# Layer-norm statistics of the linear attention taken on VectorE during the experts, its rows shared by VectorE and ScalarE

## The reference, cut to what matters

```python
x = L0_attn_x                                                   # (4, 1024, 256)
x = x + _L0_attn_ref(_layernorm(x, axis=-1), W_Q, W_K, W_V, W_O)
x = x + _L0_ffn_ref(_layernorm(x, axis=-1), ...)                # 32 experts of 128 x 128, latent width 128
x = x + _L1_attn_ref(_layernorm(x, axis=-1), ...)               # linear attention, 16 heads of 128
x = x + _L1_ffn_ref(_layernorm(x, axis=-1), ...)                # 48 kept experts, capacity 96

def _layernorm(x, axis=-1, eps=1e-05):
    m = jnp.mean(x, axis=axis, keepdims=True)
    v = jnp.var(x, axis=axis, keepdims=True)
    return (x - m) / jnp.sqrt(v + eps)
```

## Time and profile before

| | |
|---|---|
| time, median of three runs | 2960.62 us (2959.38 to 2962.0) |
| time of the profiled execution | 2959.6 us |
| span of the profiled execution | 2957.0 us |
| PE busy in the span | 2703.8 us, 91% |
| DVE busy | 1668.0 us, 56% |
| ACT busy | 1411.9 us, 48% |
| POOL busy | 789.5 us, 27% |
| phase `experts` (first to last row of DVE) | 802.4 to 1185.8 us |
| phase `lnC` (first to last row of DVE) | 1186.8 to 1222.2 us |
| first matmul of `lin` | 1233.9 us |

### The profile page before, as it was taken

How to read it: one execution, slowest core, us unless ns; L and a number is a source line. 1 busy time by engine, 2 the same in 40 slices (tenths; PEclk the granted TensorE clock), 3 DMA queues, 4 the chain that set the end, 5 groups by cost and what they waited for, 6 DMA issues and landing times. The chain is left out here.

```text
span 2957.0 us, 50661 instructions
## 1 busy us (share of the span) xinstructions
PE 2703.8 (91%) x17706; PEld 2184.6 (74%) x17706; DVE 1668.0 (56%) x3256; ACT 1411.9 (48%) x2605; POOL 789.5 (27%) x808
## 2 busy tenths in 40 slices
PE   7899999979799999599999999999999999986573
PEld 6444444468578888499998989989899998984462
DVE  7688888546588887544444444444444444448321
ACT  6477777856478777433333333333333333327210
POOL 3522221200052222122222222222222222213574
PEclk9799999989899999699999999999999999986666
DMA  8955564030154453300000000000000000004476
GB/s 253 205 98 75 73 81 67 3 98 3 54 223 185 184 184 128 116 1 1 23 1 23 1 20 4 1 23 1 23 1 1 22 1 19 1 20 143 114 166 124
DMA packets 158641, 204.14 MB, mean 69 GB/s; under 512 B 17568, under 2 KB 134976, under 8 KB 149696
## 3 DMA queue, kind: packets, MB, share of 16 engines
q1 hardware_dynamic: 149904, 186.14, 23.7%
q0 software_dynamic: 8544, 15.22, 2.9%
HBM read 154.74 MB, written 50.78 MB: 70 GB/s over the span
## 5 line engine op out<-in xcount | busy, mean ns | idle before, releaser
L1846 POOL TENSOR_TENSOR lin_o2sum<-lin_o2sum,lin_o 128x512 f32<-128x512 f32 x128 | 183.7, 1436 | 1019.5 <-ACT lin_o L1883 1019.5
L875 DVE TENSOR_REDUCE score_pm<-score_SM 128x1 f32<-128x512 f32 (+3 forms) x608 | 364.5, 657 | 80.5 <-PE score_SM L735 47.8
L829 ACT ACTIVATE score_PR<-score_SE 128x512 f32<-128x512 f32 (+1 forms) x640 | 309.8, 558 | 106.3 <-PE score_SE L763 102.6
L2101 DVE TENSOR_TENSOR C_acc<-lin_OUT,C_acc 128x512 f32<-128x512 f32 x256 | 177.1, 692 | 266.3 <-PE lin_OUT L1963 264.6
L2084 DVE SCALAR_TENSOR_TENSOR lin_go<-lin_gT,lin_O 128x512 f32<-128x512 f32 x128 | 88.0, 688 | 421.0 <-PE lin_O L1999 377.2
L1866 ACT ACTIVATE lin_qT<-lin_PJ 128x512 f32<-128x512 f32 x129 | 77.0, 597 | 433.2 <-PE lin_PJ L1925 433.2
L1925 PE MATMUL lin_PJ<-C_XH,lin_WH 128*128 128x512 f32 x774 | 253.8, 409 | 14.0 <-DVE lin_WL L2040 14.0
L1925 PE MATMUL lin_PJ<-C_XL,lin_WH 128*128 128x512 f32 x774 | 241.0, 392 | 0.0
L735 PE MATMUL score_SM<-A_KR,A_QR 96*128 96x512 bf16 (+3 forms) x768 | 229.9, 341 | 12.1 <-DVEq L81 9.4
L1925 PE MATMUL lin_PJ<-C_XH,lin_WL 128*128 128x512 f32 x774 | 240.9, 392 | 0.0
L763 PE MATMUL score_SE<-A_QR,A_KR 99*128 99x512 bf16 (+3 forms) x768 | 210.5, 330 | 2.0 <-ACT score_PR L829 1.5
(11 more groups left out here) (356 smaller groups left out, 6609.9 us busy)
## 6 DMA issues: line engine op xcount, KB each, us to landing
experts_sq<-B_roots SPq DMA_DIRECT2D x64, 1024.0 KB, 4.7
A_QR<-q_parts SPq DMA_DIRECT2D x96, 128.0 KB
A_KR<-k_parts SPq DMA_DIRECT2D x96, 128.0 KB
kept_GU<-L_ffn_gate_up_proj SPq DMA_DIRECT2D x48, 192.0 KB
v_rows<-inp_vt SPq DMA_DIRECT2D x32, 256.0 KB, 4.1
A_V<-v_rows SPq DMA_DIRECT2D x16, 512.0 KB
C_w<-L_attn_w_qkv SPq DMA_DIRECT2D x27, 256.0 KB
q_parts<-inp_parts SPq DMA_DIRECT2D x16, 384.0 KB, 3.6
```

The costliest lines, as they stand in the source:

```text
L829: nc.scalar.activation(PR[:, st % BUFS, h, 0:width], SE[:, e % RING, 0:width], ACT.Exp, scale=SCALE)\
L875: nc.vector.tensor_reduce(pm[:, n % 2, h0:h0 + nh, t, k0 // CHUNK], SM[:, count % RING, 0:nh * nk].rearrange("p (h k) -> p h k", h=nh), AX ...
L1846: nc.gpsimd.tensor_tensor(o2sum[:, c], o2sum[:, c], o2[:], ALU.add).then_inc(pool_sum, 1)
L2101: nc.vector.tensor_tensor(dst, OUT[:, half], dst, ALU.add).then_inc(dve_acc[half], 1)
```

## The change

`experts`: DVE's loop over the chunks is written out in Python, so that its semaphore counts are constants. After `low` at e = 14, 17, 20 and 23 it takes `bn_stats` of one tile of the previous chunk, and at e = 27 the four `bn_aggr`. The results `mv` and `stats` are in a PSUM tensor, `C_mv`, that lives on into `lnC`. At g = 0 the "previous chunk" is chunk 7, whose statistics are taken again later.

`lnC`: `normalise_phase` takes the place of `transpose_phase`. ACT loads the table for the root first. DVE computes the variances and scales of chunks 0 and 1 from what is there, takes the statistics of chunk 7 (`bn_stats` between variances and scales, `bn_aggr` behind the first rows), and then does the 24 tiles that are left in one go. Of each chunk's four tiles of rows ACT makes two and DVE two, both for chunk g + 2 right behind their share of chunk g. The nine DMAs of SP stay, and so do the transposes and the two buffers.

```diff
-            with dve.Fori(0, CHUNKS) as g:
+            for g in range(CHUNKS):
                 for e in range(E):
                     weigh(g, e)
@@
+                    if e in STATS_AT:                      # (14, 17, 20, 23)
+                        j = STATS_AT.index(e)
+                        t = (g + CHUNKS - 1) % CHUNKS * TPC + j
+                        dve.wait_ge(dve_x, done(2 * g + 1))
+                        dve.wait_ge(dve_mv, done(g * TPC - 1))
+                        nc.vector.bn_stats(stats[:, j, :], X[:, t, :]).then_inc(dve_stats, 1)
+                    if e == MEANS_AT:                      # 27
+                        dve.wait_ge(dve_stats, done(g * TPC + TPC - 1))
+                        for j in range(TPC):
+                            t = (g + CHUNKS - 1) % CHUNKS * TPC + j
+                            nc.vector.bn_aggr(mv[:, t, :], stats[:, j, :]).then_inc(dve_mv, 1)
@@ lnC, DVE
-            if norm:
-                variances(0)
-                scales(0)
-                variances(1)
-            for g in range(CHUNKS):
-                ... scales(run), variances(run + 1) ...
-                make_low(g)
+            variances(0)
+            for j in range(TPC):
+                nc.vector.bn_stats(stats[:, j, :], X[:, tile_of(CHUNKS - 1, j), :]).then_inc(stats_ready, 1)
+            scales(0)
+            make_rows(0)
+            dve.wait_ge(stats_ready, TPC)
+            for j in range(TPC):
+                nc.vector.bn_aggr(mv[:, tile_of(CHUNKS - 1, j), :], stats[:, j, :]).then_inc(mv_ready, 1)
+            dve.wait_ge(mv_ready, TPC)
+            variances(1)
+            make_rows(1)
+            scales(1)
+            for g in range(CHUNKS):
+                make_low(g)
+                if g + 2 < CHUNKS:
+                    make_rows(g + 2)
@@ lnC, DVE, make_rows: tiles 2 and 3 of the chunk
+                dve.wait_ge(scale_ready, 1 if g < 2 else 2)
+                for j in range(OWN, TPC):
+                    ins = nc.vector.tensor_scalar(rows[:, g % 2, j, :], X[:, t, :], rstd[:, t:t + 1],
+                                                  shift[:, t:t + 1], ALU.mult, ALU.add)
@@ lnC, ACT: tiles 0 and 1
+            act.preload_act_table(ACT.Sqrt)
+            roots(0)
+            make_rows(0)
+            make_rows(1)
+            roots(1)
+            for g in range(CHUNKS):
+                make_high(g)
+                if g + 2 < CHUNKS:
+                    make_rows(g + 2)
```

More of the change, by code:

```diff
@@ L84, with normalise_phase @@
 LH, LBLK = 16, 128
[L87 to L100, removed]
+def normalise_phase(nc, X, mv, XH, XL, ident, prefetch):
+    SPLITS = ((0, 2), (2, CHUNKS))
+    OWN = TPC // 2
+    with Phase(nc, "lnC") as ph:
+        stats = ph.sb("stats", [P, TPC, 6])
         std = ph.sb("std", [P, TILES])
@@ L115, in variances, with make_rows @@
             def variances(run):
[L116 to L127, removed]
+                nc.vector.tensor_scalar(std[:, cols_of(run)], mv[:, cols_of(run), 1], 1.0e-5, None, ALU.add)\
+                    .then_inc(var_ready, 1)
             def scales(run):
-                cols = slice(run * RT, (run + 1) * RT)
                 dve.wait_ge(std_ready, run + 1)
-                nc.vector.reciprocal(rstd[:, cols], std[:, cols]).then_inc(rstd_ready, 1)
+                nc.vector.reciprocal(rstd[:, cols_of(run)], std[:, cols_of(run)]).then_inc(rstd_ready, 1)
                 dve.wait_ge(rstd_ready, run + 1)
-                nc.vector.scalar_tensor_tensor(shift[:, cols], mv[:, cols, 0], -1.0, rstd[:, cols],
-                                               ALU.mult, ALU.mult).then_inc(scale_ready, 1)
-            give_credit(dve, low_ready)
+                nc.vector.scalar_tensor_tensor(shift[:, cols_of(run)], mv[:, cols_of(run), 0], -1.0,
+                                               rstd[:, cols_of(run)], ALU.mult, ALU.mult).then_inc(scale_ready, 1)
+            def make_rows(g):
+                if g >= 2:
+                    dve.wait_ge(transposed, g - 1)
+                dve.wait_ge(scale_ready, 1 if g < 2 else 2)
+                for j in range(OWN, TPC):
+                    t = tile_of(g, j)
+                    ins = nc.vector.tensor_scalar(rows[:, g % 2, j, :], X[:, t, :], rstd[:, t:t + 1], shift[:, t:t + 1],
+                                                  ALU.mult, ALU.add)
+                ins.then_inc(dve_rows, 1)
             def make_low(g):
@@ L159, in _ @@
         def _(pe):
[L160 to L171, removed]
+            for g in range(CHUNKS):
+                pe.wait_ge(act_rows, g + 1)
+                pe.wait_ge(dve_rows, g + 1)
+                if g >= 2:
+                    pe.wait_ge(low_ready, g - 1)
+                for k in range(KD):
+                    for j in range(TPC):
+                        ins = nc.tensor.transpose(tr[:, g % 2, k, j * P:(j + 1) * P],
+                                                  rows[:, g % 2, j, k * P:(k + 1) * P], ident[:])
+                ins.then_inc(transposed, 1)
@@ L173, in _, with roots @@
         @block.scalar
         def _(act):
-            give_credit(act, rows_ready)
+            act.preload_act_table(ACT.Sqrt)
+            def roots(run):
+                act.wait_ge(var_ready, run + 1)
+                nc.scalar.activation(std[:, cols_of(run)], std[:, cols_of(run)], ACT.Sqrt).then_inc(std_ready, 1)
             def make_rows(g):
[L178 to L197, removed]
@@ L199, in make_high @@
+                if g >= 2:
+                    act.wait_ge(transposed, g - 1)
+                act.wait_ge(scale_ready, 1 if g < 2 else 2)
+                for j in range(OWN):
+                    t = tile_of(g, j)
+                    ins = nc.scalar.activation(rows[:, g % 2, j, :], X[:, t, :], ACT.Identity,
+                                               bias=shift[:, t:t + 1], scale=rstd[:, t:t + 1])
+                ins.then_inc(act_rows, 1)
             def make_high(g):
-                act.wait_ge(transposed, done(g))
+                act.wait_ge(transposed, g + 1)
@@ L229 @@
+            roots(0)
[6 more added lines that the diff above has]
+                    make_rows(g + 2)
+RUNS = 4
+RT, RC = TILES // RUNS, CHUNKS // RUNS
 AH, AD = 16, 16
@@ L1714, in _, with latent_moe_layer @@
                 out(2 * CHUNKS + half, half)
-def latent_moe_layer(nc, a, X, AO, held, ident, out, odd, rows):
+def latent_moe_layer(nc, a, X, means, AO, held, ident, out, odd, rows):
     with ExitStack() as c:
```

74 lines of the change are left out of this document (33 added, 41 removed).

## The result

The changed kernel takes 2982.77 us (median of five runs, 2974.93 to 2984.16) against 2962.0 us (2959.38 to 2963.03) for the kernel before, measured beside it: 1.0067 times, 95% interval 1.0055 to 1.0079. The forecast was 2949.0 us and faster; it is slower by 21 us. `lnC` did get shorter, by what was forecast. The loss is in `lin`, whose code was not touched.

A forecast was written before the change was run, and what follows sets the result against it. PE sets the time in `experts`; in `lnC` DVE and ACT take turns. Terms -11.1 (`lnC`), -1.0 (clock) and +1.0 (first chunk) took 2959.6 to 2948.5 us, forecast as 2949.0; 8 in 10 range 2944.8 to 2954.

The forecast's parts named there:

- part 2: Loop of `lnC`: no run waits for statistics; `lnC` gains 11.1 us; transposes in number, barrier and start of `lin` stay.
- part 5: DVE's program: the written-out loop's code fetching costs 0, with 1.8 us kept both ways.
- Rival 4: `lnC`: the wait moves to its DMAs, gain below 11 us; 4% together with anything else, such as shifted code.
- Part 1: Head of `lnC`: table load and statistics cover each other; the first transpose comes 3.3 us earlier.
- the ring: `lnC` loop: PE transposes, ACT copies, DVE makes `C_XL` and rows, PE reuses the buffer; 4.94 us per two chunks.
- the clock: PE's granted clock in `lnC`: a shorter rest and fuller work may raise it, taken as 1.0 us gained.
- DVE's row: `lnC`: one row operation on DVE, taken as 0.346 us, with ends of 0.35 and 0.87 for two tiles.
- Part 3: PE's clock in `lnC`: possible gain of 0 to 3.9 us from a higher level, 1.0 us taken.
- Part 4: Loop of `experts`: added DVE statistics cost 0 in seven of eight chunks and 1.0 us once.
- the first chunk: `experts`: added statistics delay PE there, 1.0 us lost once, with ends of 0 and 2.3.
- Rival 3: `experts`: added statistics reach PE in every chunk, 18.4 us lost against 11.1 won, 2966.9 us; 5%.

The follow-up runs named there:

- e2: The kernel before with only PE's transpose loop in `lnC` written out; 2998.95 us, 1.0127 of the kernel before.
- p1: The kernel of e1 with ACT making all four tiles of rows of each chunk and DVE none; 2949.95 us, 0.9973 of the kernel before.
- e1: The changed kernel with PE's transposes of `lnC` in a hardware loop again; 2952.57 us, 0.9966 of the kernel before.
- e3: The changed kernel with sixteen semaphore increments added at the head of PE's part of `lin`; 2951.31 us, 0.9962 of the kernel before.
- s8_timed: The changed kernel with eight semaphore increments added at the head of PE's part of `lin`; 2951.0 us, 0.9959 of the kernel before.
- e1c: The kernel of e1 repeated unchanged; 2949.34 us, 0.9966 of the kernel before.

## Why the prediction was wrong

**The step that failed** is the sentence in part 2 that the transposes in number, the barrier and the start of `lin` stay, with part 5, which priced the fetching of DVE's code alone at 0, and 1.8 us either way. The transposes did stay in number, but not as instructions: 64 of them now stand in PE's program where sixteen stood in a loop. `lin`'s first matmul does come 12.9 us after the last `C_XL`, as before; what moved is the place of `lin`'s loop within PE's code, and it costs 31.4 us where the forecast had nothing, more than two and a half times the gain of `lnC`. Rival 4 had "a shift of code that costs in many places" as a few words in a 4% remainder, with no price. The diff on PE (a `Fori` gone) was to be seen, and so was the 0.7 to 1.3 us of "issue" that PE paid at each turn of `lin`.

The Trainium skill, "Runtime: NRT & Kernel Launch", section "Instruction fetch mechanics", says that code comes in blocks of 256 instructions, fetched one after the other, and that a taken branch out of the fetched window must wait for a fetch. The run with 240 fillers agrees with the 256. The same section holds crossing a block for mostly hidden, and unrolling for the better form. The runs differ where the block ends right behind the target of a jump: 2.2 to 2.9 us at each turn, 3.5 to 4.7 when both waits fall together, and 36 us for one loop written out (e2).

**Part 1** held: first transpose 8.9 us after the last `Y` against 12.4, so 3.5 earlier where 3.3 was forecast. From SP's first DMA (1189.81) it is 3.1 us. The table load took its 1.28 us beside the statistics.

**Part 2** held in sum. `lnC` is 12.0 us shorter (3.5 + 8.5), where 11.1 were forecast for the ring and 1.0 for the clock. DVE's row was mis-sized inside its bounds:

```profile
L135 DVE TENSOR_SCALAR lnC_rows<-X,lnC_rstd,lnC_shift x16: 403/407/415, 1191.8 to 1208.9; 128x256 f32<-128x256 f32 x16
```

0.407 us, where the row with one per-partition factor gave 0.346. At the lower clock two chunks take about 5.0 us (first transposes 1202.11 and 1207.11), where 4.94 was worked out.

**Part 3** came out inside its bounds, and that was luck. I took 1.0 of 0 to 3.9 us. The clock rose at 1197, 4.0 us after PE began at 1192.94 with nothing but transposes:

```profile
1196.00:1197.00 1.00, 0.61 (x3) 0.21 (x1) 1.00 (x1) 1.00 (x3) 0.00 (x0) 0.53 1.00 344
1197.00:1198.00 1.00, 0.03 (x1) 0.06 (x1) 0.98 (x4) 1.00 (x2) 0.00 (x0) 1.00 1.14 399
```

and fell again within the microsecond from 1200. For 3.4 us it was up, and two bursts ran faster for it: 1.07 and 1.50 us instead of 1.94, which is 1.3 us. It rose once more within the microsecond from 1210, and the first and the last burst (3.68 and 1.62 us) were some 0.6 us shorter together. In p1, whose bursts are 2.88 us apart, it did not rise: eight transposes take 1.96 us in each. The spacing is not shown to be the reason: in e2 the bursts stand as in the kernel before (first transposes at 1193.38, 1200.14, 1203.02), and the clock rose there within the microsecond from 1196, where it stayed low in the kernel before. The Trainium skill's "TensorE: Matmul & The Clock Gate", section "Part 4: PE-mode transpose", has transposes not count for the clock. By these rows the clock can rise with nothing but transposes on PE, so the rule does not hold here; that this kernel's transposes run in the mode of that section is shown in no row.

**Part 4**: the seven chunks cost nothing, as forecast; the 1.0 us of the first chunk was not there either (378.5 before, 378.0 after, 378.4 without its statistics). From 895 to 940 us, to be read against the earlier trace rows:

```profile
895.00:940.00 45.00, 45.00 (x200) 37.29 (x199) 37.91 (x66) 35.95 (x66) 10.36 (x8) 1.00 0.50 186
```

PE is busy all through, with DVE at 37.91 us instead of 37.37. One `bn_stats` took 0.428 us and one `bn_aggr` 0.163, writing to PSUM, a little over the 0.415 and 0.15 assumed. Rival 3 is out, and rival 4's DMAs too: they end by about 1210, before the last `C_XL`.

**Sum.** Without the shift of PE's code the forecast's sum is what is measured: e1, e3, s8_timed and e1c stand 9.1 to 11.6 us below their kernels before (2962.72 - 2952.57, 2962.72 - 2951.31, 2962.61 - 2951.0, 2958.47 - 2949.34), where 11.1 was worked out. These versions beat both kernels. The agreement of the single terms is weaker than that of the sum: the first chunk cost nothing instead of 1.0, and the stretches of unchanged code differ by up to 4 and 8 us between profiles.

**What stays open.** Why the next packet of code starts only half a microsecond behind the loop's first matmul, and why PE needs 1.2 to 1.5 us more after its end. Whether the next turn's weights, which come in at the same time (DMA share 0.74 and 0.49 in the rows from 1411), lengthen the packet is open too; no run took that traffic away. And why the clock rises in one run of the same bursts and not in another.

## What to carry to other kernels

Ask of every edit where it moves the code of each engine, also of engines whose work is the same: a loop written out shifts every later loop, and a later hardware loop pays at each of its turns if its head comes to lie a few instructions before the end of a fetched block. The sign is a wait with "issue" right behind a loop's head, at the same matmul in every turn. To tell it from real work, put eight or sixteen semaphore instructions ahead of the loop; here the time fell by 31 us, and the fillers are the mend as well.

## What the runs showed of the hardware

- Place of a loop's head: 0.7 to 1.3 us of wait per jump at best, and a second wait of 2.2 to 2.9 us (with 4 fillers 3.5 to 4.7 for both) if a block ends within a few instructions. Eight instructions more make 29 us less in `lin` (1438.0 and 1408.7).
- The instruction queue that follows PE's program moved packets of 16.4 KB, 0.9 to 1.6 us each in the waits of the changed kernel, and PE went on 1.2 to 1.5 us after the packet's end.
- Such a wait has a second price. PE's granted clock fell to 0.50 in it or up to 1.3 us behind it and stayed there 3.4 us, once 6.8: 1.8 of the 4.3 us per turn.
- PE's granted clock rose from 0.50 to 1.00 with nothing but transposes on PE, 4.0 us after the first of them in the changed kernel and 3.3 us in e2; in the kernel before, with the same bursts as e2, it did not.
- A semaphore instruction on PE ahead of `lin` cost 0.15 to 0.16 us between 92 and 240 of them, and 8 or 16 were not to be seen.
